# First head pair of a cross-attention kernel: another order of context splits, turns of x, residual addition, bias and normalisation, and value and key weights split behind the normalisation

## The reference

```python
x = _rmsnorm(hidden_states, ln_weight)           # hidden_states = layernorm(x)
h_q = (x @ w_q.T).reshape(b, lq, H, DH)
h_k = (key_value_states @ w_k.T).reshape(b, lk, H, DH)
h_v = (key_value_states @ w_v.T).reshape(b, lk, H, DH)
score = jnp.einsum('bqhd,bkhd->bhqk', h_q, h_k)
score = score + position_bias[None]
m = attention_mask[:, None]
score = jnp.where(m, score, -jnp.inf)
score = jax.nn.softmax(score, axis=-1)
score = jnp.where(m, score, 0.0)
attn = jnp.einsum('bhqk,bkhd->bqhd', score, h_v).reshape(b, lq, H * DH)
out = attn @ w_out.T
return hidden_states + out
```

## Time and profile before

| what | value |
|---|---|
| three runs | 1738.42, 1743.58, 1744.41 us |
| profiled execution, its own time | 1740.23 us |
| its span | 1738.4 us |
| mean granted clock of TensorE | 0.987 |
| busy: TensorE, VectorE, GpSimd, ScalarE | 96%, 52%, 39%, 37% |
| TensorE busy, 50 to 110 us | 53.08 of 60 us |
| TensorE busy, 250 to 400 us | 150.00 of 150 us |

### The profile page before, as it was taken

How to read it: one execution, slowest core, us unless ns; L and a number is a source line. 1 busy time by engine, 2 the same in 40 slices (tenths; PEclk the granted TensorE clock), 3 DMA queues, 4 the chain that set the end, 5 groups by cost and what they waited for, 6 DMA issues and landing times. The chain is left out here.

```text
span 1738.4 us, 26186 instructions
## 1 busy us (share of the span) xinstructions
PE 1677.0 (96%) x9412; PEld 1449.2 (83%) x9412; DVE 912.4 (52%) x1462; ACT 642.2 (37%) x1757; POOL 685.3 (39%) x480
## 2 busy tenths in 40 slices
PE   8899999999999999999989998799999999999997
PEld 7788888888888888888868886688888788888875
DVE  5734454443544434443454346556657556665674
ACT  5422233221332223332222222455546545564550
POOL 4532343333433324433253433445435434443524
PEclk9999999999999999999989999899999999999998
DMA  5111100111101111011011110201011110010011
GB/s 177 52 52 51 51 20 32 51 51 51 46 5 51 51 51 51 0 51 57 1 51 50 47 38 25 65 31 37 31 38 43 44 37 31 25 43 25 24 38 49
DMA packets 30898, 74.99 MB, mean 43 GB/s; under 512 B 5776, under 2 KB 10256, under 8 KB 30832
## 3 DMA queue, kind: packets, MB, share of 16 engines
q1 hardware_dynamic: 30832, 74.10, 12.2%
HBM read 71.99 MB, written 2.10 MB: 43 GB/s over the span
## 5 line engine op out<-in xcount | busy, mean ns | idle before, releaser
L1761 POOL TENSOR_TENSOR g_swapped<-g_swapped,rawB 128x512 f32<-128x512 f32 x80 | 103.5, 1295 | 159.3 <-ACT g_swapped L1545 159.3
L631 ACT COPY x_pT<-banks 128x512 f32<-128x512 f32 x64 | 37.5, 586 | 337.6 <-PE banks L485 337.6
L920 POOL TENSOR_TENSOR wtV_lo<-rawV,wtV_hi 128x1024 fp32r<-128x1024 f32 x16 | 38.5, 2406 | 309.6 <-ACT wtV_hi L643 309.6
L55 PE MATMUL banks<-wtV_hi,cT_lo 128*128 128x256 f32 x512 | 145.1, 283 | 0.0
L57 PE MATMUL banks<-wtV_hi,cT_hi 128*128 128x256 f32 x512 | 144.8, 283 | 0.0
L56 PE MATMUL banks<-wtV_lo,cT_hi 128*128 128x256 f32 x512 | 144.7, 283 | 0.0
L934 POOL TENSOR_TENSOR x_probs<-x_probs,x_inv 128x512 f32<-128x512 f32 x64 | 66.8, 1044 | 158.0 <-DVE x_inv L769 155.1
L55 PE MATMUL banks<-wtV_hi,g_att_lo 128*128 128x512 f32 x256 | 106.2, 415 | 8.1 <-DVE g_att_lo L1659 8.1
L777 DVE COPY x_v<-banks 128x512 f32<-128x512 f32 x60 | 41.5, 692 | 127.7 <-PE banks L57 127.7
L623 ACT ACTIVATE x_probs<-x_probs,x_top 128x128 f32<-128x128 f32 x256 | 99.2, 390 | 18.8 <-DVE x_top L760 18.8
L801 DVE TENSOR_TENSOR resid<-banks,resid 128x512 f32<-128x512 f32 x128 | 84.1, 686 | 40.0 <-PE banks L57 40.0
(11 more groups left out here) (226 smaller groups left out, 4953.2 us busy)
## 6 DMA issues: line engine op xcount, KB each, us to landing
rawV<-in_x_wV SPq DMA_DIRECT2D x16, 512.0 KB, 4.3
rawO<-in_x_wO SPq DMA_DIRECT2D x16, 512.0 KB, 6.0
rawO<-in_g_wQ SPq DMA_DIRECT2D x16, 512.0 KB, 3.2
rawV<-in_g_wO SPq DMA_DIRECT2D x16, 512.0 KB, 3.2
rawA<-in_x_wA SPq DMA_DIRECT2D x15, 512.0 KB, 6.3
rawB<-in_x_wB SPq DMA_DIRECT2D x15, 512.0 KB, 5.0
rawA<-in_f_gu SPq DMA_DIRECT2D x5, 512.0 KB, 3.7
rawB<-in_f_gu SPq DMA_DIRECT2D x5, 512.0 KB, 3.1
```

Of the source, the lines that this page charges most:

```text
L55: pe.matmul(out, w[1], x[0], start=start, stop=False)
L631: nc.scalar.copy(pT[:, j, :], banks[:, TURN_BANK + j, :]).then_inc(pT_ready, 1)
L920: pool.tensor_tensor(wt[kind][1][:, :], raw[kind][:, :], f32(wt[kind][0][:, :]), ALU.subtract)\
L1761: pool.tensor_tensor(part, part, sin[:, :].unsqueeze(1).to_broadcast([P, HB, P]), ALU.mult)\
```

## The change

Seven edits, all in `cross_attention_phase`:

- ScalarE's `start` rounds all four context chunks before B's key half, and V's first tile before it copies the first keys. It takes up the turned batches (`high`) at the head of each round, before the scaling of the next two.
- TensorE's `start` transposes two batches of x before, not behind, the values of each round.
- `add_hidden` moves from VectorE, where its eight instructions stood among the first head pair's logits and inverses, to ScalarE, ahead of the first exponentials. It is an `Identity` activation with scale and bias there, so GpSimd makes `-mean * rstd` by one more instruction.
- On VectorE `inverse(0, 0)` comes ahead of `logits(0, 1)`.
- GpSimd makes these factors before the mask and the first bias, not behind them.
- GpSimd splits the V and B tiles of pair g in `body(g)`, behind the two normalisations of head 2g-1 and the bias, not at the end of the stretch before.
- SyncE's `body` loads V and B before the bias.

```diff
                 def body(g, first, last):
                     load("A", g)
-                    bias(g)
                     load("V", g)
                     load("B", g)
+                    bias(g)
                     load("O", g)
...
                     for n in range(4):
-                        values_of(n, V0 + n)
                         turn_x(2 * n)
                         turn_x(2 * n + 1)
+                        values_of(n, V0 + n)
...
+                def add_hidden(b):
+
+                    act.wait_ge(twice_ready, 1)
+                    nc.scalar.activation(resid[:, b, :], resid[:, b, :], ACT.Identity, bias=mean_scaled[:, b:b + 1],
+                                         scale=twice[:, b:b + 1]).then_inc(hidden_added, 1)
+
                 def start():
                     key_half("A")
-                    context(0)
-                    context(1)
+                    for c in range(DC):
+                        context(c)
                     key_half("B")
-                    context(2)
-                    context(3)
+                    weights("V", 0)
                     for half in range(2):
                         keep(k_[:, 0, half * HALF:(half + 1) * HALF], K_A0 + half)
-                    weights("V", 0)
                     scale_x(0)
                     scale_x(1)
...
                     for n in range(4):
+                        high(2 * n)
+                        high(2 * n + 1)
                         if n < 3:
                             scale_x(2 * n + 2)
...
                         keep_values(n)
-                        high(2 * n)
-                        high(2 * n + 1)
+                    for b in range(B):
+                        add_hidden(b)
                     exps(0, 0)
...
-                def add_hidden(b):
-
-                    dve.wait_ge(twice_ready, 1)
-                    dve.tensor_scalar(resid[:, b, :], resid[:, b, :], twice[:, b:b + 1], mean_scaled[:, b:b + 1],
-                                      ALU.mult, ALU.subtract).then_inc(hidden_added, 1)
...
-                    pool.tensor_tensor(mean_scaled[:, :], core.moments[:, :, 0], core.rstd[:, :], ALU.mult).then_inc(twice_steps, 1)
+                    pool.tensor_tensor(core.var_eps[:, :], core.moments[:, :, 0], core.rstd[:, :], ALU.mult).then_inc(twice_steps, 1)
                     pool.wait_ge(twice_steps, 3)
+                    pool.tensor_scalar(mean_scaled[:, :], core.var_eps[:, :], -1.0, None, ALU.mult).then_inc(twice_steps, 1)
+                    pool.wait_ge(twice_steps, 4)
```

More of the change, by code:

```diff
@@ L859, in start @@
                     logits(0, 0)
-                    for b in range(2):
-                        add_hidden(b)
+                    inverse(0, 0)
                     logits(0, 1)
                     query(Q_B0, 0, 1)
-                    inverse(0, 0)
-                    for b in range(2, 4):
-                        add_hidden(b)
                     inverse(0, 1)
                     query(Q_B0 + 1, 1, 1)
-                    for b in range(4, B):
-                        add_hidden(b)
                     attn_lo(0, 0, 0)
@@ L976, in start @@
                     query_half("B")
+                    twice_of()
                     pool.wait_ge(mask_in, DMA)
@@ L982, in start @@
                     bias(0, 0, True)
-                    twice_of()
                     normalise(0, 0)
@@ L988, in start @@
                     weights("O", 0)
-                    weights("V", 1)
-                    weights("B", 1)
                 def body(g, first, last):
@@ L996, in body @@
                     bias(a, 0)
+                    weights("V", g)
+                    weights("B", g)
                     normalise(a, 0)
@@ L1002, in body @@
                     bias(a + 1, 1)
-                    if not last:
-                        weights("V", g + 1)
-                        weights("B", g + 1)
                 start()
```

## The result

The changed kernel takes 1731.91 us (median of four runs, 1730.75 to 1733.36), the kernel before 1741.9 us over its four runs. The ratio is 0.9944 with a 95% interval of 0.9923 to 0.9966: about 9.8 us or 0.56% faster. 1734 was forecast, with a range of 1729 to 1740.5. In a second set of runs the same kernel came out at 0.9936 (0.9923 to 0.9950). The profiled execution took 1732.21 us, its span 1730.4 us against 1738.4.

The account below looks back on a forecast made before the run. TensorE, busy in 96% of the span, bound the kernel, so only its waits could pay. -0.74, -6.16 and -1.82 gave -8.7 us: 1731.5 from the profiled 1740.2, 1734.9 from the median 1743.6; forecast 1734, range 1729 to 1740.5.

Parts of the forecast that it names:

- Front: TensorE's start, up to the first query product: context wait gone (-0.5), partly offset by scaling and switch costs; gain 0.1 us.
- First head pair: TensorE's first pair of heads: the 1.0 us wait goes and the body begins at 54.8 instead of 55.56, -0.74 us.
- The long wait: TensorE's 6.0 us wait for normalised probabilities in the first turn goes entirely; transposition at 63.83 instead of 69.99, -6.16 us.
- the undisturbed piece: TensorE's three projections in the loop's next turn, 117.04 to 125.31, taken as the measure without a wait: 8.27 us.
- Slow clock: TensorE's piece between the first turn's two transpositions returns from 5.03 to 3.21 us at full clock, -1.82 us.
- Additions: Eight residual additions as ScalarE activations, 0.65 us each, 5.2 in all, hidden before the exponentials with 1.5 us of cover.
- Later turns: Turns after the first: earlier normalisation gains nothing, later V split loses nothing, its low half ready 11.8 us in.
- Rival C: Every turn: moved GpSimd splits collide with VectorE's copies, logits and maxima, making it slower, 1749.5 at 1.2 us each; chance 0.07.
- Sum: All terms together, first head pair, long wait and slow clock: -8.7 us.
- A: Cover too thin at the normalisation or turns of x: 2 us of wait remain without slow clock, 1737; chance 0.16.
- B: The wait only moves: normalisation still behind a whole split, 3 us wait and 1.8 slow clock stay, 1739.5; chance 0.09.

Follow-up runs that it names:

- e1: The kernel before with only SyncE's loads of V and B ahead of the bias and GpSimd's V and B splits moved later; ratio 0.9966.
- e2: The kernel before with only the additions on ScalarE, their factors made ahead of the mask and the first inverse ahead of the second logits; ratio 0.9999.
- e3: The changed kernel with GpSimd's splits of V and B back ahead of the normalisations; 1734.33 us in one run.
- e4: The changed kernel with SyncE's bias load back ahead of the loads of V and B; 1738.51 us in one run.
- e7: The changed kernel with TensorE waiting for V only behind two turns of x, and head 1's second-half scores ahead of head 0's second transposition; ratio 0.9939.
- e8: The changed kernel itself, run again in a second set of runs; ratio 0.9936.

## Why the prediction was right

- **Front, 0.1 us forecast: 0.5, by luck.** TensorE's first matmul started 0.74 us earlier in this profile (7.48 against 8.22); from there to the first query product it took 28.57 us before and 28.82 after. Piece by piece, the wait for the context shrank from 0.46 us to 0.19 where I had forecast none, and the last two scalings ran at 31.32, not 31.8, so no turn of x waited for them. A wait I had not seen came, 0.43 us for V's low half ahead of the first turns, whose code waits for V though the turns don't need it.
- **First head pair, -0.74 with 0.1 of the front in it: -1.28 with 0.49.** The pair's own part is 0.79 us against 0.64, by the mechanism as described.
- **The long wait, -6.16: -6.16.** 62.55 - 54.28 = 8.27, the undisturbed piece, so nothing was left of it; GpSimd was done at 60.63 with 1.9 us of slack, as forecast. e1 to e4 show that both causes had to go, and that the order of SyncE's loads is the largest one: with all else in place it is worth 6.3 us of the interval, the additions with what goes with them 4.6, the place of the splits 1.5.
- **Slow clock, -1.82: -1.81** (3.22 us between the transpositions).
- **Additions, 5.2 us with 1.5 of cover: 5.76 with 0.95.** Under the 0.85 each that I had called the limit. No table was loaded ahead of them: ScalarE's rows show none between 2 and 813 us. So the trace agrees with what the Trainium skill ("ScalarE: Activation LUTs", on table sets) says of identity.
- **Later turns, no gain or loss: exactly none**, 696.19 us either way, and V's split in the first turn ends at 66.85, 12.6 us in, against 11.8 forecast and 15 as the limit. Rival C is refuted by that and by the rows of 0.69 us under the splits.
- **Sum: -8.7.** The interval, which the start doesn't move, is 8.76 us shorter, against 8.62 forecast without the front. With the start's luck TensorE was 9.2 us ahead in the second turn. In code that did not change this lead went up and down. It is 10.0 us behind the feed-forward layer (1077.41 against 1067.37), and 8.9 behind the border to the grouped attention (1121.45 against 1112.60): both kernels have nearly the same waits there, but the slow level behind them lasts longer in the changed one (a clock of 0.50 from 1091.6 to 1093.6, where the kernel before has 1.00 at the same place). The lead is 8.3 us near the end, and the span is 8.0 shorter.
- **The time.** The four-run medians lie 9.99 us apart, and the ratio's interval, 0.9923 to 0.9966, stands for 6 to 13 us, so the runs can't tell 8.7 from 10. The forecast of 1734 stood on a median of three runs, 1743.6; the four runs give 1741.9, and 8.7 less is 1733.2, against 1731.91 measured.

Rivals A and B did not occur: nothing waited for probabilities where the long wait had been, nor for a scale at the turns of x; and e3, which puts the normalisation behind both splits again as B has it, waits only 1.28 us at full clock. A's price was mis-sized: I had written that 2 us of wait would cost 2, "without the slow clock". e1 has just that wait and pays 1.62 us more. The chances were 0.44 for faster by more than 0.5% and 0.50 for within it, on a forecast that lay on the line. The measured ratio, 0.9944, is just past the line and its interval holds it, so the result decides between the two no better than the forecast did.

## What to carry to other kernels

When TensorE waits, follow the wait back until every branch of it ends, and look for a second branch that ends nearly as late. Removing one alone gains less than its share of the whole (here 0.35 and 4.1 us, where both gave 8.7). In a queue that runs in order, a transfer that waits for a late buffer delays all behind it; one moved line in SyncE's list was worth 6.3 us. And once the waits left in the changed code are down to half a microsecond, one later fall of the clock (1.46 us in e7) can outweigh what removing them gives, so the times no longer tell.

## What the runs showed of the hardware that I had not expected

- **The price of the slow clock does not follow the length of the wait.** At one and the same place, in one profile each: a wait of 1.28 us cost nothing more, 2.13 cost 1.62 us, 4.52 cost 1.62, 5.34 cost 2.82 and 6.00 cost 1.82. Behind the two longest the transposition is slow at once (its four instructions take 1.11 us); behind the other three it takes 0.65, as at full clock, and with 2.13 and 4.52 us the clock falls only after it.
- **The same wait need not have the same price.** In e8 and e7 a wait of 1.76 us at one place, and the same 7.9 us up to its end (TensorE busy for 6.16 us, clock 1.00), was followed by a clock of 1.00 in one and of 0.50 in the other, which cost 1.46 us.
- **What a GpSimd instruction holds up on VectorE depends on the operands.** The four additions (input and output in SBUF) took 8.45 us under GpSimd's work, where the first two of the eight took 1.00 together in the same profile; a multiplication of 4 columns, 0.16 us by itself, took 1.2 to 1.8 us; copies and logits out of PSUM and row maxima took 0.69 us under the same splits.
